# Where in a round a graph-attention kernel on one core computes the row numbers of its list gathers

## What is computed

```python
h = jnp.maximum(_layernorm(x, axis=-1), 0.0)
h = jnp.einsum('ni,hif->hnf', h, W)                  # 8 heads of 64
s1, s2 = einsum('hnf,hf->hn', h, a1), einsum('hnf,hf->hn', h, a2)
scores = leaky_relu(s1[:, :, None] + s2[:, None, :], 0.2)
scores = jnp.where(adj[None] > 0, scores, -9e15)
att = softmax(scores, axis=-1)
out = jnp.einsum('hnm,hmf->hnf', att, h)             # heads side by side
return x + elu(out)
```

## Time and profile before

| | us |
|---|---|
| median of 3 runs | 788.54 |
| the three runs | 784.62, 788.54, 789.19 |
| the profiled execution, whole | 785.17 |
| span of its profile | 783.6 |
| VectorE busy | 650.9 (83%) |
| TensorE busy | 568.1 (73%) |
| ScalarE busy | 477.8 (61%) |
| GpSimd busy | 421.9 (54%) |

### The profile page before, as it was taken

The page is one execution under the profiler, slowest core; times in us unless marked ns, Lnnn a source line. Parts: engine busy times, 40 slices in busy tenths (PEclk is TensorE's granted clock), DMA queues, the critical chain, the costliest instruction groups (busy, mean ns, idle before and its releaser), DMA issues.

```text
span 783.6 us, 9125 instructions
## 1 busy us (share of the span) xinstructions
PE 568.1 (73%) x2182; PEld 405.0 (52%) x2182; DVE 650.9 (83%) x1969; ACT 477.8 (61%) x761; POOL 421.9 (54%) x802
## 2 busy tenths in 40 slices
PE   0489789898887777834687656877588659898763
PEld 0245445554444444414566445665466548776652
DVE  4659989999976657954799879999899998999883
ACT  0678887799999979715556546666556314334322
POOL 4634434454333323226767436666747776887860
PEclk9989999999999998965788869777778879998986
DMA  8999999999999999805999999999999887899995
GB/s 279 421 383 396 398 389 379 405 387 420 417 417 419 423 419 423 355 21 190 404 408 415 414 393 321 397 396 401 402 390 374 241 203 188 220 240 289 300 260 162
DMA packets 62395, 269.50 MB, mean 344 GB/s; under 512 B 12050, under 2 KB 12050, under 8 KB 49876
## 3 DMA queue, kind: packets, MB, share of 16 engines
q1 hardware_dynamic: 33524, 185.81, 58.8%
q0 software_dynamic: 25824, 77.31, 32.6%
q10 hardware_dynamic: 2992, 5.77, 2.0%
HBM read 243.49 MB, written 31.13 MB: 350 GB/s over the span
## 4 chain that ended last, share of the span: by engine, by line
DVE 23%; DMA 10%; POOL 9%; issue 9%; ACT 4%; PE 0%; DVEq 0%; POOLq 0%
DVE nodes L1157 9%; DMA nodes<-table,list_column 9%; POOL nodes L990 5%; POOL nodes L985 3%; DVE agg L1169 3%; DVE places L270 2%; ACT result L1049 2%; ACT result L1047 2%; DVE best L259 2%; DVE to_row L1133 1%; DVE result L1177 1%; DMA nodes<-table,column 1%; DVE owner L1098 1%; POOL out_dram L972 1%; PE psC L1288 0%
## 5 line engine op out<-in xcount | busy, mean ns | idle before, releaser
L672 PE MATMUL psH<-sb_W,normedT 128*128 128x512 f32 x384 | 223.0, 672 | 0.0
L249 ACT ACTIVATE packed<-adj_rows,eight 128x3072 uint8<-128x3072 int32 x66 | 188.7, 2858 | 0.8
L985 POOL DMA_INDIRECT nodes<-table,column x138 | 138.0, 1000 | 72.4 <-issue 40.4
L1304 PE MATMUL psP<-nodes,ident 128*128 128x256 f32 x276 | 108.1, 481 | 49.5 <-issue 43.2
L990 POOL DMA_INDIRECT nodes<-table,list_column x109 | 110.0, 1009 | 54.5 <-issue 29.3
L1157 DVE TENSOR_TENSOR nodes<-nodes,psW 128x2048 f32<-128x2048 f32 (+4 forms) x66 | 138.7, 2142 | 0.0
L719 POOL TENSOR_TENSOR sb_node_sum<-sb_node_sum,h_rows 128x512 f32<-128x512 f32 x48 | 61.2, 1274 | 132.2 <-ACT h_rows L637 132.2
L673 PEld LDWEIGHTS psS<-sb_Wa,normedT 128*128 128x128 f32 x384 | 78.1, 203 | 102.1 <-issue 102.1
L270 DVE FIND_INDEX8 places<-best,packed 128x8 uint32<-128x96 f32 (+6 forms) x240 | 110.0, 466 | 0.0
L259 DVE MAX8 best<-packed 128x8 f32<-128x96 f32 (+6 forms) x240 | 102.8, 460 | 4.0 <-ACT packed L249 3.9
L1305 PE MATMUL psP<-nodes,ident 128*128 128x264 f32 x276 | 104.0, 465 | 0.0
(11 more groups left out here) (180 smaller groups left out, 880.1 us busy)
## 6 DMA issues: line engine op xcount, KB each, us to landing
adj_rows<-in_adj_dram SPq DMA_DIRECT2D x66, 1536.0 KB, 10.9
sb_adj_rows<-in_adj_dram SPq DMA_DIRECT2D x30, 1536.0 KB, 14.9
table<-h_rows SPq DMA_DIRECT2D x48, 260.0 KB, 10.0
sb_x_rows<-in_x_dram SPq DMA_DIRECT2D x48, 256.0 KB, 10.3
out_dram<-in_x_dram SPq DMA_DIRECT2D x11, 512.0 KB, 11.8
result<-in_x_dram POOLq DMA_DIRECT2D x11, 512.0 KB, 7.9
out_dram<-result ACTq DMA_DIRECT2D x11, 512.0 KB, 4.9
out_dram<-result POOLq DMA_DIRECT2D x6, 512.0 KB, 6.9
```

Source lines behind the costliest of these rows:

```text
L249: nc.scalar.activation(words.bitcast(mybir.dt.uint8), sb["adj_rows"][buffer_of(i)][:], ACT.Square, bias=sb["eight"][:], scale=-17.0, accum ...
L672: nc.tensor.matmul(psH[:, t % 2], normedT[:, t % 2, kc], sb["W"][:, kc], start=(kc == 0), stop=(kc == KC - 1))
L985: nc.gpsimd.indirect_dma_start(out=nodes[:, node_at[u] + i * w.direct + j], out_offset=None, in_=table, in_offset=bass.IndirectOffsetOnAxi ...
L1304: nc.tensor.matmul(low, sb["ident"][:], nodes[:, n, 0:LOW], start=a, stop=False)
```

## The change

In each round, the four instructions of `front` for unit u + 3 now stand between `turn(u + 2)` and `normalise`, and no longer at the head of round u + 1, behind `normalise` and the search. `front(2)` stands ahead of the loop. In round 19, `place_late` stands behind `score_edges(19)` and no longer at the round's end, since `front(22)` now comes in that round and needs a look-up that waits for `late_planned`. No instruction is added or left out. Lines of `attend_edges` behind the loop's head move by one number at most.

```diff
--- before.py
+++ after.py
@@ -1245,14 +1245,17 @@
             own(2)
             front(1)
             turn(1)
+            front(2)
             for u in range(U):
-                front(u + 2)
                 score_edges(u)
+                if u == COUNTED + 1:
+                    place_late()
                 own(u + 3)
                 if u >= 2 and UNITS[u - 2].last:
                     finish(UNITS[u - 2].group)
                 weigh(u)
                 turn(u + 2)
+                front(u + 3)
                 if u >= 1 and UNITS[u - 1].last:
                     normalise(UNITS[u - 1].group)
                 for (t, n), r in zip(dve_items, dve_round):
@@ -1261,8 +1264,6 @@
                 if u == COUNTED:
                     rank_last(nc, dve, sb, TILES - 1)
                     count_late()
-                if u == COUNTED + 1:
-                    place_late()
             finish(UNITS[U - 2].group)
             normalise(UNITS[U - 1].group)
             finish(UNITS[U - 1].group)
```

## The result

| | before | changed |
|---|---|---|
| median, 20 runs each, side by side | 785.04 | 791.14 |
| lowest, highest | 780.12, 791.75 | 785.75, 796.43 |
| profiled execution | 785.17 | 791.31 |
| span of its profile | 783.6 | 789.6 |

Changed over before is 1.0064 (95%: 1.0040 to 1.0087), so the change costs 5.0 us (3.1 to 6.8); between the two profiled executions it is 6.1. That is slower, clear of noise, and still inside 1%. (One run of before, at 1311 us, is left out of the highest; the median without it is 784.82.)

A forecast was written before the change was run, and what follows sets the result against it. Gathers and VectorE were taken to bound the search rounds, the loop through `normalise` and `grow` the later ones. Terms 0 + 7.6 - 0.5 + 0 = +7.1 us on 786.9 gave 794 us, range 785 to 801.

The forecast's parts named there:

- Part 1: Search rounds: earlier lists end GpSimd's waits, but VectorE's gather waits gain 0 us, bounds -11.1 and +1.5.
- The sign I had named: VectorE's waits for gathers between 390 and 600 us would still be about 11 us in the new profile.
- a line in the queue that doesn't run empty: Search rounds: gathers always stand in a line of some 10 to 25 us, so earlier issue ends no sooner.
- landing times would grow by what GpSimd gained: Sign for the search rounds: gathers issued sooner would take that much longer to land; GpSimd waits were 1.6 to 4.0 us.
- the minima that I quoted for the line: Shortest gather landings, 9.8 us in 396 to 470 us and 8.1 in 480 to 600, read as a never-empty line.
- Part 2: Rounds without a search: `front` ahead of `normalise` no longer covers `grow`, lengthening rounds by its time, +7.6 us.
- Part 3: Round 19's earlier `place_late` and `front(22)`: `finish` starts 0.5 us sooner, -0.5 us, bounds -1.8 and +1.
- The 0.5 us wait ahead of L1231: Sign at `place_late` in round 19: VectorE would wait some 0.5 us for TensorE's sum.
- Part 4: `front` waiting for its facts by the end of `turn(u + 2)`: 0 us, upper bound +4, tightest 0.9 us to spare.
- the gathers gain all 11.1 us: Rival at GpSimd's list blocks of units 6, 14 and 16: all gather waits go, 783 us; 12 in 100.
- The worse tail: Rival in rounds 20 to 30: TensorE's clock falls, look-ups late, `front` waits for facts, 799 to 800 us; 14 in 100.
- nothing changes: Rival in the tail: `grow` isn't what `finish` waits for, so time stays at 787 us; 8 in 100.

The follow-up runs named there:

- kernel 2: Kernel before with `front` early in rounds 0 to 17 only, the rest and `place_late` as before; ratio to before 0.9988, -0.9 us.
- kernel 5: Kernel before with `front(u + 2)` of rounds 0 to 17 moved later, behind `turn(u + 2)`; ratio to before 1.0085, +6.7 us.
- kernel 1: Kernel before with `front` early from round 18 on only, and `place_late` early; ratio to before 1.0055, +4.3 us.
- Kernel 3: Kernel before with only `place_late` moved early, every `front` at the head of its round; ratio to before 0.9978, -1.7 us.
- kernel 4: Changed kernel with `front` and `normalise` swapped, so `normalise` stands ahead of `front(u + 3)`; ratio to before 0.9991, -0.7 us.
- kernel 7: Changed kernel with `grow` in one activation instead of two, clamp left out, so output not the layer's; ratio to before 0.9909, -7.1 us.
- kernel 13: Kernel before with one-step `grow` (clamp left out, output not the layer's) and `place_late` early; ratio to before 0.9959, -3.2 us.
- 11: Changed kernel, from round 20 `grow` of unit u - 2 right behind the exponentials, ahead of facts, `finish` behind `weigh`; ratio to before 0.9980, -1.6 us.
- 12: Kernel 4, from round 20 `grow` of unit u - 2 right behind the exponentials, ahead of facts, `finish` behind `weigh`; ratio to before 1.0003, +0.2 us.
- kernel 6: Kernel before with `grow` in one activation instead of two, clamp left out, so output not the layer's; ratio to before 0.9998, -0.2 us.

## Why the prediction was right

The forecast was +7.1 us, 0.9%, from the tail alone. Measured: +5.0 (3.1 to 6.8) in time, +6.0 in span.

**Part 1, the gathers of the search rounds: taken as 0, and near to it.** The sign I had named, waits of still about 11 us between 390 and 600 us, came (12.0), but it was a poor sign, since round 1 slides in and out of that window. By rounds 1 to 17 the six kernels with late lists have 12.6 to 16.0 us of gather waits, mean 14.4, and the eight with early ones, the changed kernel among them, 11.2 to 14.5, mean 12.7; rounds 0 to 17 take 236.4 to 239.9 us, mean 238.2, against 234.5 to 238.0, mean 236.2. So some 2 us may be gained, of the 11.1 at most, with ranges that overlap; kernel 2's time, -0.9 (-3.4 to +1.5), can't tell it from none. The reason given, a line in the queue that doesn't run empty, is borne out by kernel 5, in which gathers issued later landed sooner after their issue. That landing times would grow by what GpSimd gained showed in the minima only. And the minima that I quoted for the line leave out 470 to 480 us, which lies between the two windows. In before, the gathers of that gap have

```profile
DMA to landing us min/median/max: 3.6/7.5/10.8
```

so the line had all but run out there. GpSimd's wait ahead of these gathers was not for a list but 12.7 us for TensorE's sum that frees the ring, and an earlier list doesn't shorten that wait. The conclusion stands; the reading that the minima show a line everywhere doesn't.

By the formula of the Trainium skill's page "DMA: Bandwidth & Descriptors", section "Anatomy of one DMA — SWDGE (gpsimd) path", 2.0 us plus bytes over 436 GB/s, a block would take 2.6 us, an estimate; none in the search windows above took under 5.3, and the shortest between them was 3.6.

**Part 2, the tail: +7.6 foreseen, +7.2 in rounds 20 to 30 of the changed kernel's profile, +7.6 in kernel 1's.** The waits for `grow` were to go to about 19 us; they went to 20.3, and in the ten rounds that the sum names, 21 to 30, from 3.7 to 11.6, +7.9. Kernels 2 and 3, without it, have 92.8 and 92.1 us there, and kernel 4, with `front` behind `normalise`, 92.1. The mechanism, cover turned into series, is shown twice more. With `grow` in one step and `place_late` early, rounds 20 to 30 take 89.1 us with `front` where the change puts it (kernel 7) and 89.0 with `front` at the head of the round (13); with `grow` first, 91.8 and 92.9 with `front` ahead of `normalise` and behind it (11 and 12). Once `grow` is out of the way, its place costs nothing.

**Part 3, `place_late`: -0.5 foreseen.** From the start of round 17, `finish` of round 20 starts 40.9 us later in before and 40.1 in the changed kernel: -0.9. The 0.5 us wait ahead of L1231 did not come in the changed kernel, since TensorE's sum was in time; it was 0.72, 1.43 and 0.40 us in kernels 1, 3 and 4, and 0 to 1.30 in the others with the early step. Kernel 3 alone is -1.7 (-4.4 to +1.0). Inside the bounds given, and a little better than the value taken. What I missed is that the early step also frees TensorE's sums and with them GpSimd's ring, which kernel 13 showed.

**Part 4, facts: 0.** No wait ahead of L1110 inside the loop. The tightest places have more than 1.5 us to spare, more than the 0.9 foreseen.

**The size.** From round 17 on the changed kernel's profile has 7.2 - 1.2 + 0.7 = +6.7 us, where 7.1 were foreseen. The 0.7 behind the start of round 30 holds the last of the ten rounds of part 2: the wait ahead of `finish` in round 30, 0.84 us before and 1.61 now, lies there. The timed +5.0 is less, with 6.7 just inside its interval, and kernel 1 is timed at +4.3 (2.3 to 6.4) where its stretches give about +8. For the changed kernel some 2 us gained in rounds 0 to 17 would close the gap, but kernel 1, whose lists are late there, can't be explained so. Nor do the times show such a gain: of kernels that differ in little but the lists of the search rounds, early over late is +0.7 us (changed over 1), +1.0 (4 over 3) and -0.9 (2 over before), each within noise. Why the times are 2 to 4 us under the profiles is open. Profiles of one kind differ by 3 us in rounds 0 to 17 alone, so that +7.1 and +5.0 lie close says less for the account than the stretches do. Of the 2.9 us between the 794 and the 791.14 measured, 1.9 is the time taken for before (786.9 from four runs, 785.04 over twenty).

**The rivals.** That the gathers gain all 11.1 us (783) fell by kernels 2 and 5. The worse tail (799) fell: there were no waits for facts, and the tail grew by no more than part 2 says. The granted clock of rounds 20 to 30 did come out lower, 0.89 against 0.92 before, but kernel 1 has the whole loss at 0.94. That nothing changes (787) fell with the interval.

## What to carry to other kernels

Work on one engine that lies between a request to another engine and the use of its answer is cover: moved ahead of the request, it costs its full length in every round in which that answer was already late, though not one instruction was added. A long wait on an engine that fills a queue is worth little so long as the queue itself has work; before counting such waits as gain, look at the shortest time from issue to landing, over the whole stretch and without gaps between windows, and at the engine's other waits, which may take over what one of them gives up. Add up the waits by unit, not by a window of time into which a wait can slide. And when a wait on the critical path is removed, look for the next one at once: here GpSimd, whose lead over VectorE falls to some 3 us in the tail of kernel 6, took back all that a shorter `grow` gave.

## What the runs showed of the hardware

GpSimd's gathers move at a quarter of their own pace while a load of adj is under way. Queue by queue in 4 us of the kernel before, first with such a load all through (424 to 428 us), then without (460 to 464 us), and last from 390 to 600 us: packets, MB, share of the 16 engines.

```profile
q1 hardware_dynamic: 120, 1.28, 77.0%
q0 software_dynamic: 115, 0.38, 23.4%
```

```profile
q0 software_dynamic: 488, 1.54, 104.5%
```

```profile
q0 software_dynamic: 11343, 35.62, 47.3%
```

0.38 MB are 1.4 blocks of 266 KB in 4 us, while GpSimd can issue one each 1.25 us. Over 390 to 600 us it is 0.68 MB in 4 us, 44% of the pace alone, as loads come and go. That fits the landing times of up to 30 us, and that little that GpSimd does sooner helps.

And from kernel 5: the state in which GpSimd leaves a stretch matters for the next. Where the gathers stood in line, later lists cost between nothing and 3 us, and took 6 us of GpSimd's lead (21.3 to 15.2 us for unit 20). Behind that, where gathers land in 3.6 to 6.4 us, the kernel's profile has 5.3 us of loss.
